# Ranks from a running count kept per image, narrower Q passes, and the early tile table summed on GpSimd, in an attention and mixture-of-experts kernel on one Trainium2 core

## What is computed

```python
h = h + attention(layernorm(h))          # Q = elu(x Wq)+1, K, V; out = Q (K^T V) / (Q sum K)
x = layernorm(h)
logits = x @ gate_w.T
sel, rw = argmax(logits), sigmoid(max(logits))
for e in range(8):                       # each token is in one expert only
    xs = x * (rw * (sel == e))[:, None]
    out = out + (xs @ w_up[e].T) * silu(xs @ w_gate[e].T) @ w_down[e].T
h = h + out
```

## Time and profile before

| what | value |
|---|---|
| three runs | 437.87 us median (436.64 to 438.05) |
| the profiled execution | 436.53 us, its span 434.7 us |
| TensorE busy, share of span | 412.7 us, 95% |
| VectorE busy | 349.8 us, 80% |
| GpSimd busy | 298.6 us, 69% |
| ScalarE busy | 283.1 us, 65% |
| mean granted TensorE clock | 0.989 of full speed |

### The profile page before, as it was taken

The page is one execution under the profiler, slowest core; times in us unless marked ns, Lnnn a source line. Parts: engine busy times, 40 slices in busy tenths (PEclk is TensorE's granted clock), DMA queues, the critical chain, the costliest instruction groups (busy, mean ns, idle before and its releaser), DMA issues.

```text
span 434.7 us, 13221 instructions
## 1 busy us (share of the span) xinstructions
PE 412.7 (95%) x4325; PEld 398.7 (92%) x4325; DVE 349.8 (80%) x1147; ACT 283.1 (65%) x688; POOL 298.6 (69%) x678
## 2 busy tenths in 40 slices
PE   7999999999999999999999999999997999999980
PEld 6999899999999999999999999989896998999970
DVE  5678568999999999999999999998886766766650
ACT  5554476788688788788778778766664554555530
POOL 4065214677878888888888888776677777666662
PEclk9999999999999999999999999999999999999995
DMA  7974122333422321231311211128612797222120
GB/s 268 348 250 146 52 48 57 95 93 94 115 71 67 90 68 40 66 96 39 111 53 36 59 55 40 51 74 226 185 45 69 235 288 238 98 73 72 70 78 14
DMA packets 34148, 46.46 MB, mean 107 GB/s; under 512 B 8842, under 2 KB 25856, under 8 KB 34082
## 3 DMA queue, kind: packets, MB, share of 16 engines
q1 hardware_dynamic: 24860, 30.50, 23.2%
q0 software_dynamic: 9216, 15.12, 11.1%
q10 hardware_dynamic: 6, 0.00, 0.0%
HBM read 26.87 MB, written 17.17 MB: 101 GB/s over the span
## 4 chain that ended last, share of the span: by engine, by line
PE 85%; DVE 5%; issue 4%; ACT 1%; DMA 1%; POOL 1%; POOLq 0%; SPq 0%; DVEq 0%
PE b_kg L1400 8%; PE b_kg L1401 8%; PE b_kg L1402 8%; PE b_w L1400 7%; PE b_w L1401 7%; PE b_w L1402 6%; PE b_att L1515 6%; PE b_t L1465 3%; PE b_w L1701 3%; PE b_v L1402 3%; PE b_v L1400 3%; PE b_v L1401 3%; PE b_att L1701 3%; PE b_att L1452 3%; PE b_t L1529 3%
## 5 line engine op out<-in xcount | busy, mean ns | idle before, releaser
L674 POOL DMA_INDIRECT sorted_rows<-rows,place x64 | 75.5, 1180 | 20.3 <-issue 9.4
L760 POOL DMA_INDIRECT out<-result,rows_all x64 | 62.3, 973 | 28.4 <-DVE result L1308 14.7
L866 ACT ACTIVATE q_exp<-b_w,bq_s 128x228 f32<-128x228 f32 x64 | 28.9, 452 | 28.6 <-PE b_w L1402 28.6
L1400 PE MATMUL b_kg<-wgu_hi,xsT_hi 128*128 x128 | 41.3, 323 | 0.5 <-issue 0.4
L1296 DVE SCALAR_TENSOR_TENSOR act_u<-b_kg,rows_all,silu_g 128x128 f32<-128x128 f32 x64 | 19.4, 345 | 27.1 <-ACT silu_g L961 26.7
L1400 PE MATMUL b_w<-xnT_hi,wq_hi 128*128 128x264 f32 x128 | 39.5, 309 | 1.3 <-DVE logits L1119 1.0
L1400 PE MATMUL b_kg<-wkgv_hi,xnT_hi 128*114 128x264 f32 x128 | 38.7, 302 | 0.4 <-DVE patch_out L1036 0.4
L1401 PE MATMUL b_kg<-wkgv_lo,xnT_hi 128*114 128x264 f32 x128 | 36.5, 285 | 0.0
L1401 PE MATMUL b_w<-xnT_lo,wq_hi 128*128 128x264 f32 x128 | 36.4, 285 | 0.0
L1402 PE MATMUL b_kg<-wkgv_hi,xnT_lo 128*114 128x264 f32 x128 | 36.4, 284 | 0.0
L1402 PE MATMUL b_w<-xnT_hi,wq_lo 128*128 128x264 f32 x128 | 36.4, 284 | 0.0
(11 more groups left out here) (233 smaller groups left out, 1561.7 us busy)
## 6 DMA issues: line engine op xcount, KB each, us to landing
rows_all<-sorted_rows SPq DMA_DIRECT2D x64, 130.0 KB, 3.2
rows_all<-in_x SPq DMA_DIRECT2D x18, 384.0 KB, 4.7
rows_all<-in_txt SPq DMA_DIRECT2D x32, 154.0 KB
rows_all<-in_wgu_in SPq DMA_DIRECT2D x8, 256.0 KB, 3.0
rows_all<-patch_out SPq DMA_DIRECT2D x48, 36.0 KB
sorted_rows<-tail_rows SPq DMA_DIRECT2D x9, 130.0 KB, 2.9
sorted_rows<-rows,place POOLq DMA_INDIRECT x64, 3.7
wdown<-in_wdown_in SPq DMA_DIRECT2D x2, 512.0 KB, 4.5
```

The costliest lines, as they stand in the source:

```text
L674: G.indirect_dma_start(out=scratch[0:EXPERTS * REGION, :], out_offset=bass.IndirectOffsetOnAxis(ap=place[:, k, b:b + 1], axis=0), in_=rows ...
L760: G.indirect_dma_start(out=out, out_offset=bass.IndirectOffsetOnAxis(ap=rows_all[:, t.n, ID:ID + 1].bitcast(I32), axis=0), in_=result[:, k ...
L866: S.activation(q_exp[:, c, :], at, ACT.Exp, bias=bq_s[:, c:c + 1])
L1400: T.matmul(to, left_hi, right_hi, start=start, stop=False, skip_group_check=seeded)
```

## The change

Four things change. (1) GpSimd keeps one running count per image: `so_far[:, half, 0]` is the count before the pair, `so_far[:, half, 1]` is that plus image 0's `chosen`, made by a first add of 8 columns; a second add of 8 makes row 0 of the other half. `rank` then needs two products, and it waits for the first add of its own pair (`so_far_ready` 2p+1), where it waited for the count of the pair before. The products that read the counts for the tables are single ones. (2) In TensorE's `queries` only the first of the six passes of each half still writes 264 columns, the other five write 256. (3) The early table's product and sums leave VectorE; GpSimd makes them in three halving adds each, after `count_chosen` in its steps 28 and 29. (4) In GpSimd's tail `count_chosen(PAIRS - 1)` stands ahead of `scatter(PAIRS - 2)`.

```diff
@@ -401,6 +401,9 @@
         early_pe = sem("early_pe")
         early_chain = sem("early_chain")
         early_ready = sem("early_ready")
+        early_ends_ready = sem("early_ends_ready")
+        early_past_ready = sem("early_past_ready")
+        early_slot_step = sem("early_slot_step")
         stored = [sem(f"stored{k}") for k in range(RESULT_RING)]
         SMALL_DMAS, WEIGHT_DMAS = 1, 7
@@ -653,10 +656,12 @@
                 pool.wait_ge(chosen_ready, p + 1)
                 if p >= 1:
+                    pool.wait_ge(so_far_ready, 2 * p)
                     pool.wait_ge(rank_done, p)
-                    pool.wait_ge(so_far_ready, p)
-                G.tensor_tensor(so_far[0:TOK, (p + 1) % 2], so_far[0:TOK, p % 2], chosen[:, p % 2],
-                                ALU.add).then_inc(so_far_ready, 1)
+                now, then = so_far[0:TOK, p % 2], so_far[0:TOK, (p + 1) % 2]
+                G.tensor_tensor(now[:, 1], now[:, 0], chosen[:, p % 2, 0], ALU.add).then_inc(so_far_ready, 1)
+                pool.wait_ge(so_far_ready, 2 * p + 1)
+                G.tensor_tensor(then[:, 0], now[:, 1], chosen[:, p % 2, 1], ALU.add).then_inc(so_far_ready, 1)
             def scatter(p):
@@ -682,6 +687,34 @@
                 pool.wait_ge(gu_hi_done, n + 1)
                 G.tensor_tensor(wgu_lo[:, e, k, :], gate_up_raw(e)[:, k, :], wgu_hi[:, e, k, :].bitcast(F32), ALU.subtract).then_inc(gu_lo_done, 1)
+            def over_slots(ap):
+                return ap.rearrange("p (a e) -> p a e", a=1).to_broadcast([1, EARLY_TILES, EXPERTS])
+
+            def early_link(ins, count):
+
+                ins.then_inc(early_slot_step, 1)
+                pool.wait_ge(early_slot_step, count)
+
+            def early_past():
+
+                pool.wait_ge(early_past_ready, 1)
+                early_link(G.tensor_tensor(past_n[:], past[:], over_slots(ends[:, 0, EXPERTS:2 * EXPERTS]), ALU.mult), 1)
+
+            def early_sums():
+
+                for n, width in enumerate((EXPERTS // 2, EXPERTS // 4, EXPERTS // 8)):
+                    G.tensor_tensor(past[:, :, 0:width], past[:, :, 0:width], past[:, :, width:2 * width], ALU.add)
+                    early_link(G.tensor_tensor(past_n[:, :, 0:width], past_n[:, :, 0:width], past_n[:, :, width:2 * width], ALU.add), 2 + n)
+
+            def early_rows():
+
+                early_link(G.tensor_scalar(slot_r[:], past_n[:, :, 0], -float(P), None, ALU.mult), 5)
+                early_link(G.tensor_tensor(slot_r2[:], slot_r[:], slots_s[:, EARLY_TILES * EXPERTS:], ALU.add), 6)
+                early_link(G.tensor_scalar(slot_s[:], past[:, :, 0], float(REGION), None, ALU.mult), 7)
+                early_link(G.tensor_tensor(slot_r[:], slot_s[:], slot_r2[:], ALU.add), 8)
+                G.tensor_copy(slot_row[:, 0:EARLY_TILES], slot_r[:])
+                G.tensor_copy(slot_expert[:, 0:EARLY_TILES], past[:, :, 0]).then_inc(early_ready, 1)
+
             def step(i):
                 if 0 <= i - 3:
                     rstd2_of(i - 3)
@@ -692,6 +725,11 @@
                 if 0 <= i - 3:
                     top_value(i - 3)
                     count_chosen(i - 3)
+                if i == EARLY_PAIRS + 5:
+                    early_past()
+                if i == EARLY_PAIRS + 6:
+                    early_sums()
+                    early_rows()
                 if i in GU_SPLIT_STEPS:
                     gate_up_low(GU_SPLIT_STEPS.index(i))
@@ -745,8 +783,8 @@
             scatter(PAIRS - 3)
             rstd2_of(PAIRS - 2)
             top_value(PAIRS - 2)
+            count_chosen(PAIRS - 1)
             scatter(PAIRS - 2)
-            count_chosen(PAIRS - 1)
             rstd2_of(PAIRS - 1)
             top_value(PAIRS - 1)
             scatter(PAIRS - 1)
@@ -1159,7 +1197,7 @@
                 V.tensor_reduce(first[:], ranked[:], AX_X, ALU.max).then_inc(first_ready, 1)
                 dve.wait_ge(first_ready, p + 1)
                 if p >= 2:
-                    dve.wait_ge(so_far_ready, p - 1)
+                    dve.wait_ge(so_far_ready, 2 * (p - 1))
                     dve.wait_ge(rank_done, p - 1)
                 V.tensor_tensor(chosen[:, p % 2], ranked[:],
                                 first[:].rearrange("p (b a) -> p b a", a=1).to_broadcast([TOK, 2, EXPERTS]),
@@ -1197,28 +1235,19 @@
                 dve.wait_ge(early_pe, 2)
                 dve.wait_ge(kvm_done, EARLY_PAIRS + 5)
-                V.tensor_copy(ends[:, 0], early_ends)
-                early_link(V.tensor_scalar(early_f[:, 1:2], early_before, -1.0, float(EARLY_TILES), ALU.mult, ALU.add), 4)
+                V.tensor_copy(ends[:, 0], early_ends).then_inc(early_ends_ready, 1)
+                V.tensor_scalar(early_f[:, 1:2], early_before, -1.0, float(EARLY_TILES), ALU.mult, ALU.add).then_inc(early_chain, 1)
+
+            def early_share():
+
+                dve.wait_ge(early_chain, 4)
+                V.scalar_tensor_tensor(early_f[:, 2:3], early_f[:, 1:2], 0.0, early_f[:, 0:1], ALU.max, ALU.min).then_inc(early_chain, 1)
+                dve.wait_ge(early_ends_ready, 1)
+                V.tensor_tensor(past[:], slots_s[:, 0:EARLY_TILES * EXPERTS].rearrange("p (t e) -> p t e", t=EARLY_TILES),
+                                over_slots(ends[:, 0, 0:EXPERTS]), ALU.is_ge).then_inc(early_past_ready, 1)
             def over_slots(ap):
                 return ap.rearrange("p (a e) -> p a e", a=1).to_broadcast([1, EARLY_TILES, EXPERTS])
-
-            def early_slots():
-
-                early_link(V.scalar_tensor_tensor(early_f[:, 2:3], early_f[:, 1:2], 0.0, early_f[:, 0:1], ALU.max, ALU.min), 5)
-                early_link(V.tensor_tensor(past[:], slots_s[:, 0:EARLY_TILES * EXPERTS].rearrange("p (t e) -> p t e", t=EARLY_TILES),
-                                           over_slots(ends[:, 0, 0:EXPERTS]), ALU.is_ge), 6)
-                V.tensor_reduce(slot_e[:], past[:], AX_X, ALU.add)
-                early_link(V.tensor_tensor(past_n[:], past[:], over_slots(ends[:, 0, EXPERTS:2 * EXPERTS]), ALU.mult), 7)
-
-            def early_rows():
-
-                early_link(V.tensor_reduce(slot_s[:], past_n[:], AX_X, ALU.add), 8)
-                early_link(V.scalar_tensor_tensor(slot_r[:], slot_s[:], -float(P), slots_s[:, EARLY_TILES * EXPERTS:],
-                                                  ALU.mult, ALU.add), 9)
-                early_link(V.scalar_tensor_tensor(slot_r2[:], slot_e[:], float(REGION), slot_r[:], ALU.mult, ALU.add), 10)
-                V.tensor_copy(slot_row[:, 0:EARLY_TILES], slot_r2[:])
-                V.tensor_copy(slot_expert[:, 0:EARLY_TILES], slot_e[:]).then_inc(early_ready, 1)
             def step(i):
                 if 0 <= i - 1:
@@ -1229,12 +1258,10 @@
                     early_ends_out()
                 if 0 <= i - 4:
                     places(i - 4)
-                if i == EARLY_PAIRS + 5:
-                    early_slots()
-                if i == EARLY_PAIRS + 6:
-                    early_rows()
                 if 0 <= i - 2:
                     attention_low(i - 2)
+                if i == EARLY_PAIRS + 5:
+                    early_share()
                 if 0 <= i - 1:
                     queries(i - 1)
                 if 0 <= i + 2 < PAIRS:
@@ -1331,6 +1358,7 @@
             def late_count():
                 dve.wait_ge(table_pe, 1)
+                dve.wait_ge(early_chain, 5)
                 V.tensor_copy(tail_at[:], region_ends).then_inc(table_ready, 1)
                 table_link(V.tensor_scalar(held_i[:, 0:1], region_end, con["c_regcol"][:, 0:1], float(P - 1), ALU.subtract, ALU.add), 1)
                 table_link(V.tensor_scalar(held_i[:, 1:2], held_i[:, 0:1], P.bit_length() - 1, None, ALU.logical_shift_right), 2)
@@ -1340,6 +1368,7 @@
             def late_slots():
                 dve.wait_ge(table_pe, 2)
+                dve.wait_ge(early_ready, 1)
                 table_link(V.tensor_copy(ends[:, 1], tile_ends), 5)
                 table_link(V.tensor_tensor(past[:], slots_s[:, 0:EARLY_TILES * EXPERTS].rearrange("p (t e) -> p t e", t=EARLY_TILES),
                                            over_slots(ends[:, 1, 0:EXPERTS]), ALU.is_ge), 6)
@@ -1417,8 +1446,7 @@
             def rank(p):
                 pe.wait_ge(chosen_ready, p + 1)
-                if p >= 1:
-                    pe.wait_ge(so_far_ready, p)
+                pe.wait_ge(so_far_ready, 2 * p + 1)
                 if p < PAIRS - 3:
                     pe.wait_ge(attn_ready, p + 3)
                 elif p == PAIRS - 3:
@@ -1431,11 +1459,7 @@
                     pe.wait_ge(logits_ready, PAIRS)
                 ranks = rank_bank(p)
                 T.matmul(ranks, earlier[:], chosen[:, p % 2].rearrange("p b e -> p (b e)"), start=True, stop=False)
-                T.matmul(ranks[:, EXPERTS:], ones_bf[0:TOK, :], chosen[:, p % 2, 0, :], start=False, stop=False)
-                for b in range(2):
```

(29 more changed lines are left out.)

## The result

The changed kernel takes 451.22 us (median of four runs, 450.0 to 451.93) against 437.44 us before (the three runs of above and a fourth): a ratio of 1.031, 95% interval 1.029 to 1.034. That is slower by 13.8 us; the forecast was 7 slower, with 451 as its upper end. The profiled execution took 451.93 us with a span of 450.1, against 434.7 before: 15.4 us more.

The account below looks back on a forecast made before the run. TensorE's issue bound the kernel before (8.25 us a step); the new wait would close two loops near 8.6. Rank(27) at +9.9, then tail credits, gave +7.0: 443.5 profiled, 444.9 us on the median's basis; range 438.5 to 451.

Parts of the forecast that it names:

- loop B: GpSimd alone, count to count in the 16 steps with a weight split: 8.62 us a step, bounds 8.39 and 8.78.
- The wait it adds: Rank waits for its own pair's first add: rank(1) not before 87.09, 0.92 us later, and paid again through two loops.
- R(1): R(p) is the start of rank(p); for pair 1 the forecast was 87.09, +0.92 us against before.
- Loop A: Through TensorE, VectorE and GpSimd: 17.26 us for two ranks, 8.63 a step, or 8.44 without the 0.39 stretch.
- The full stretch beside VectorE: A GpSimd instruction lengthened beside VectorE's L1097, by shared-port locking: 0.39 us in full, staying in most steps.
- What the change takes off TensorE: Two rank products fewer save 0.13 us, narrower Q passes 0.03 to 0.04: a TensorE-set step of 8.09 us.
- The early table: Sums moved to GpSimd behind count(25) and count(26): 3.9 us for sums and rows, bounds 3.0 and 5.0.
- The whole 2.45 goes: In the tail, count(31) queued ahead of pair 30's scatters ends before rank(31), removing TensorE's wait of 2.45 us.
- TensorE is full after that: Behind the removed tail wait TensorE stays busy, so a credit of 2.8 us was taken.
- TensorE's clock is no rival: The clock stays at 1.00, the full 2.4 GHz, as over the present 2.45 us wait; no cost in the sum.
- the high bound: Slow end: steps 8.63 and 8.78, table 5.0 and 0.8; R(27) +14.1, end +11.8, 449.7 us.
- GpSimd becomes the bound throughout, with the stretch full: Rival: all steps set by GpSimd, VectorE locked out in turn; 448 to 452 us, chance 0.17.

Follow-up runs that it names:

- experiment 2: The kernel before with the new counts alone (two adds, two rank products, rank waits for its own pair): 449.85 us, ratio 1.028.
- experiment 3: The changed kernel with top_value and count_chosen ahead of rstd1_of in each GpSimd step: 446.41 us, ratio 1.021 to the kernel before.
- experiment 11: The changed kernel with VectorE's qT instruction reading one input instead of two (relu half left out of the result): 445.69 us, ratio 1.020.
- Experiment 5: The kernel before with only count_chosen(31) moved ahead of scatter(30) in GpSimd's tail: 437.35 us, ratio 1.000.
- experiment 8: The changed kernel with the old counts, and ScalarE's duo_step(3) put ahead of centred(31) and tanh(31): 431.62 us, ratio 0.986 to the kernel before.
- experiment 9: The changed kernel with ScalarE's duo_step(3) put ahead of centred(31) and tanh(31) in the tail: 447.19 us, ratio 1.021 to the kernel before.
- experiment 6: The kernel before with only the Q passes narrowed to 256 columns after the first: 436.69 us, ratio 0.997.
- experiment 7: The kernel before with only the early table's sums moved to GpSimd: 436.12 us, ratio 0.997.
- experiment 4: The changed kernel with two adds kept, but rank in three products that wait for the pair before: 441.03 us, ratio 1.008 to the kernel before.

## Why the prediction was wrong

The two loops are the ones forecast, but loop B was sized too small, and the credit for the tail and the clock taken as constant were wrong: +7.0 against +15.4 in the profiled pair (+13.8 in medians). Step by step:

- **The wait it adds.** R(1) = 86.99 for 87.09. Right, to 0.1 us.
- **Loop A.** 8.66 a step for 8.63. Right; most of the 0.03 is that an add starts 0.30 ahead of its rank and not 0.26. Experiments 2 and 3 show the loop: present with the counts alone, gone when the add comes earlier.
- **Loop B.** This term was mis-sized. "I take 8.62, between": it measured 8.82, just over the bound of 8.78. Over 16 steps that is 3.2 us. The full stretch beside VectorE comes in 27 of 32 steps (L645 over 0.55 in 18, L671 over 0.5 in 9), where I took 0.23 of the 0.39 (it is 0.45). The reason I gave (GpSimd's chain will start near where L1097 lies) spoke for the full one. Since a rank starts a fixed 0.30 us after its count, and `qT` follows the rank, both engines now meet at the same place in every step; experiment 11 shows the stretch to set the step.
- **What the change takes off TensorE.** Two products instead of four: 0.17 us for the rank (104.30 to 104.47) where it was 0.26, so 0.09 for a forecast 0.13. No matter here, for TensorE is not the bound. By the 25 ns of the Trainium skill (TensorE: Matmul & The Clock Gate, "Wait — 56ns, not 53.3ns?") it would be 0.05; the rows lie between the two.
- **The early table.** R(26) to R(27) grew by 1.85 us for 2.0, but by luck: the table took 4.3 us for 3.9, and from its end to count(27) GpSimd took 5.37 us (311.14 to 316.51) for 5.97, because L671 met neither `qT` there (0.19 us, 0.54 before) nor a wait for ScalarE's `tanh_top` (0.24 before). Between R(23) and R(26) the gain was 0.1 us (26.71 for 26.81) where I credited 0.6: another 0.5. GpSimd sets these steps, and two things are missing in my loop: the 0.94 us of L671 beside the comparison and `qT`, and the product (L701), which I priced at 0.8 and put in no line of the sum.
- **"The whole 2.45 goes", "TensorE is full after that."** This step failed, by 2.4 us. The wait went and 2.74 us came back at L1727. I followed the count and not what else stood behind the two scatters on GpSimd: the second normalisation of pair 31, on which ScalarE waits in front of the experts' activations. Experiment 5 shows it alone, at no gain; experiments 8 and 9 remove it and gain 2.9 and 4.0 us.
- **"TensorE's clock is no rival."** This step failed too. Behind waits of 1.80 and 2.74 us the granted clock was 0.59 and 0.58 for some 4 us each. By experiment 9 they cost 1.5 and about 0.9 us, where the sum had nothing. I argued from one execution in which a wait of 2.45 left the clock at 1.00.
- **Slips in the working.** From +14.1 at R(27), the tail's -2.9 gives +11.2 and not the +11.8 of the high bound. And for rank never to wait, loop A as written needs GpSimd's chain under 6.5 us (two steps of 8.09 less 9.46 and 0.26), not under 6.9; in experiment 3 it is 5.76, and there the waits are gone. Neither moves the forecast.

From R(27) on the forecast had -2.9 and the trace +1.9: the tail's wait and the clock make up these 4.8 us of the miss. Loop B is 3.2, the three steps from R(23) 0.5, loop A 0.2, and R(1) and the step to R(27) -0.3 together. That is the 8.4 us between forecast and trace. The rival "GpSimd becomes the bound throughout, with the stretch full" was right in the steps with L688, but not in the others, where GpSimd still waits 0.65 us. Its range of 448 to 452 holds the 451.22 by luck: loop B at its full size adds 3.2 us to the 444.9, which is 448.1, and the rest is tail and clock.

What stays open: why one execution gets the lower clock behind a wait and another does not. No run shows either what separates the one-input form of `qT`, which holds GpSimd, from L1087, which has one input too and does not.

## What to carry to other kernels

A result that an engine reads one step late is slack, even if the engine that makes it looks idle a fifth of the time: before a reader is moved onto this step's value, add up the whole loop that the new wait closes, over as many steps as it spans. Parts of a change don't have fixed prices: moving the table was worth -1.6 us while GpSimd's chain was slack and +2.1 once the ranks waited for it, a good part of that by the lower clock behind the longer wait. And when an item is pulled out of a queue behind a long transfer, look at what else is queued there, for the wait goes to the next one: here the gain came only when ScalarE's order was changed as well.

## What the runs showed of the hardware

The lower clock is not a matter of the wait's length alone. Experiments 6 and 7 have the same wait of 2.46 us at the last count as the kernel before has the earlier trace rows, here in experiment 6,

```profile
330.26 0.19 PE L1738 MATMUL b_att<-so_far,ones_bf 128*1 128x8 bf16 x2 [2.46 <-POOL so_far L658]
```

and both show the lower clock around it, where the profile of the kernel before has 1.00. The stretches of experiment 6, with the granted clock third from the end:

```profile
328.00:332.00 4.00, 1.74 (x12) 1.71 (x13) 0.94 (x3) 0.41 (x1) 3.37 (x8) 0.73 0.25 63
332.00:336.00 4.00, 3.96 (x27) 3.52 (x27) 2.73 (x14) 2.65 (x8) 2.40 (x7) 0.85 0.24 83
```

The mean granted clock of whole executions goes with their times: among 54 of the kernel before, the 17 with 0.983 took 438.6 us in the mean, the 10 with 0.988 or 0.989 took 437.0. The profiled one, of 436.53, had 0.989. So the 1.3 us by which the median lies above it is of the size of one such stretch, which a forecast from one trace can't see.

VectorE and GpSimd can hold each other up, and the one that starts first is not slowed. `qT` ahead of a GpSimd instruction made that one 0.64 us long instead of 0.19; GpSimd's L688 ahead of `qT` made `qT` 1.09 instead of 0.62 (experiment 4).

Two small instructions on GpSimd, the second waiting for the first, start 0.27 to 0.28 us apart (253.30, 253.57), and two that do not wait 0.15 apart (255.82, 255.97).
